# Decode on 16 bit words, value splits and finish moved, a later stack, six exponential places

## The reference

```
x = x + 0.5 * ffn(layernorm(x)); x = x + attention(layernorm(x)); x = x + 0.5 * ffn(layernorm(x))
ffn: w_gu, w_down = fp4 values (8 in an int32, table 0 .5 1 1.5 2 3 4 6 and signs) * fp16 scales per 128
     h = silu(x @ gate.T) * (x @ up.T)  (1408 wide);  y = h @ w_down.T;  y / sqrt(mean(y*y) + 1e-6)
attention: another layer norm with gain and bias; Q, K, V = Xn @ W + b; 16 heads of 32;
     causal softmax(Q K.T / sqrt(32)) @ V;  @ Wo + bo
```

## Time and profile before

| | us |
|---|---|
| median of 3 runs | 2748.12 (2747.58 to 2749.52) |
| profiled execution | 2745.77, its span 2744.0 |
| PE busy | 2589.1 (94%) |
| DVE busy | 1935.7 (71%) |
| POOL busy | 1510.9 (55%) |
| ACT busy | 1475.2 (54%) |

### The profile page before, as it was taken

One profiled execution on the slowest core, in us unless ns is written; L12 is line 12 of the kernel. 1 busy time (PEld: TensorE's weight loads), 2 busy tenths in 40 slices (PEclk: granted clock), 3 DMA queues, 4 the chain that ended last, 5 costly groups with the idle time before them and its releaser, 6 DMA issues.

```text
span 2744.0 us, 39443 instructions
## 1 busy us (share of the span) xinstructions
PE 2589.1 (94%) x14559; PEld 1361.4 (50%) x14559; DVE 1935.7 (71%) x3379; ACT 1475.2 (54%) x2834; POOL 1510.9 (55%) x1061
## 2 busy tenths in 40 slices
PE   5799999999898999999999989999999999999998
PEld 3455555555673333333278723333334555555554
DVE  7987777767647877777475577777764877777765
ACT  3366666665323566666622246656665466666664
POOL 4556666665322566666342236666662556666665
PEclk8999999999999999999999999999999999999999
DMA  2002311121023020200050210202002501111101
GB/s 63 1 31 93 127 47 47 47 93 47 31 57 70 6 50 4 65 5 3 3 199 31 71 42 6 48 6 64 6 3 102 196 16 47 47 47 47 47 31 47
DMA packets 78016, 136.34 MB, mean 50 GB/s; under 512 B 19551, under 2 KB 24698, under 8 KB 77694
## 3 DMA queue, kind: packets, MB, share of 16 engines
q1 hardware_dynamic: 77822, 133.81, 15.7%
HBM read 71.12 MB, written 34.34 MB: 38 GB/s over the span
## 4 chain that ended last, share of the span: by engine, by line
PE 70%; DVE 11%; POOL 5%; ACT 5%; issue 4%; SPq 2%; DMA 1%; POOLq 0%; DVEq 0%; ACTq 0%
PE pp L96 55%; PE ps L96 14%; DVE sb L117 5%; POOL sb L105 5%; ACT sb L102 5%; DVE sb L111 4%; SPq L138 2%; PE ps L99 1%; DVE sb L105 1%; DVE sb L108 0%; DMA sb<-sb 0%; DMA sb<-xc 0%; PE pp L99 0%; DVE sb L123 0%; DVE sb L114 0%
## 5 line engine op out<-in xcount | busy, mean ns | idle before, releaser
L96 PE MATMUL pp<-sb,sb 128*128 128x512 f32 (+10 forms) x11128 | 2199.9, 439 | 64.3 <-DVE sb L105 15.1
L105 POOL TENSOR_TENSOR sb<-sb,sb 128x512 f32<-128x512 f32 (+6 forms) x1042 | 1503.2, 1464 | 1220.4 <-ACT sb L102 422.2
L96 PEld LDWEIGHTS pp<-sb,sb 128*32 128x32 f32 (+4 forms) x11128 | 1076.0, 131 | 930.5 <-issue 369.6
L102 ACT ACTIVATE sb<-pp 128x512 f32<-128x512 f32 (+5 forms) x1394 | 667.1, 550 | 457.9 <-PE pp L96 427.7
L96 PE MATMUL ps<-sb,sb 128*128 128x512 f16 (+7 forms) x2888 | 758.8, 350 | 59.0 <-DVE sb L111 22.3
L117 DVE TENSOR_REDUCE sb<-ps 128x1 f32<-128x512 f32 (+3 forms) x772 | 492.5, 668 | 151.2 <-PE ps L96 148.6
L102 ACT ACTIVATE sb<-sb 128x512 fp32r<-128x512 f32 (+4 forms) x515 | 308.5, 605 | 516.5 <-DVE sb L111 368.0
L96 PEld LDWEIGHTS ps<-sb,sb 128*128 128x128 f16 (+4 forms) x2888 | 241.0, 101 | 397.7 <-DVE sb L117 104.8
L111 DVE SCALAR_TENSOR_TENSOR sb<-ps,sb,sb 128x512 f32<-128x512 f32 x437 | 320.5, 748 | 132.1 <-PE ps L96 100.9
L111 DVE SCALAR_TENSOR_TENSOR sb<-pp,sb,sb 128x512 f32<-128x512 f32 x447 | 324.3, 746 | 109.2 <-PE pp L96 106.5
L117 DVE TENSOR_REDUCE sb<-pp 128x1 f32<-128x512 f32 (+3 forms) x348 | 232.6, 668 | 88.4 <-PE pp L96 87.9
(11 more groups left out here) (26 smaller groups left out, 398.0 us busy)
## 6 DMA issues: line engine op xcount, KB each, us to landing
sb<-sb SPq DMA_DIRECT2D x144, 128.0 KB, 2.4
sb<-L_attn_X SPq DMA_DIRECT2D x64, 256.0 KB, 3.4
sb<-xa SPq DMA_DIRECT2D x64, 256.0 KB, 4.6
sb<-xc SPq DMA_DIRECT2D x64, 256.0 KB, 3.5
xa<-sb SPq DMA_DIRECT2D x32, 256.0 KB, 2.0
xc<-sb SPq DMA_DIRECT2D x32, 256.0 KB, 5.1
out<-sb SPq DMA_DIRECT2D x32, 256.0 KB, 2.0
dd<-sb SPq DMA_DIRECT2D x11, 512.0 KB, 5.7
```

The source lines that it names most:

```text
L96: return self.e.matmul(*a, **k) if self.e else self
L102: return self.e.activation(*a, **k) if self.e else self
L105: return self.e.tensor_tensor(*a, **k) if self.e else self
```

## The change

Six edits. (1) `decode_dve` works on 16 bit words with immediates, and the mask constants and their wait go. (2) In batch 0 the four splits of Wv stand ahead of the tail's squares. (3) The finish of the last tile of the first feed-forward part is one fused VectorE instruction for each block of 128 tokens, as it already was in the second part; `features_dve` waits for it. (4) The second stack comes behind the rows of query tile 1 on SP's list, not of query tile 0. (5) ScalarE's keep waits for the stacks of its own head group alone. (6) From step 120 on, exponentials have six places, two of them in memory that the stack of head group 2 used; the first use of these waits for the last exponential of head group 2.

```diff
-    u = p.pk[:, :, :].rearrange("p a b -> p (a b)").bitcast(U32)[:, 192 * i:192 * i + 192]
+    u = p.pk[:, :, :].rearrange("p a b -> p (a b)").bitcast(U16)[:, 384 * i:384 * i + 384]
-            e.scalar_tensor_tensor(p.t1[m % 2][:, :].bitcast(U32), u, 12 - 4 * m, sign, ALU.logical_shift_left,
-                                   ALU.bitwise_and).then_inc(*p.V.up())
+            e.tensor_scalar(p.t1[m % 2][:, :], u, 12 - 4 * m, 0x8000, ALU.logical_shift_left,
+                            ALU.bitwise_and).then_inc(*p.V.up())
...
-            e.scalar_tensor_tensor(p.vv[:, m, half].bitcast(U32), u, abs(sh), size,
+            e.tensor_scalar(p.vv[:, m, half], u, abs(sh), 0x0E00,
...
-            e.scalar_tensor_tensor(v, v, 0, p.t1[(m - 1) % 2][:, :].bitcast(U32), ALU.logical_shift_left,
-                                   ALU.bitwise_or).then_inc(*p.V.up())
+            e.tensor_tensor(v, v, p.t1[(m - 1) % 2][:, :], ALU.bitwise_or).then_inc(*p.V.up())
...
-        elif what == "last" and not f.final(at[0]):
+        elif what == "last" and at[0] < NT - 1:
...
-        elif what == "last" and f.final(at[0]):
+        elif what == "last" and at[0] == NT - 1:
...
-            e.scalar_tensor_tensor(x, f.Y[tb], p.r4[:, tb:tb + 1], x, ALU.mult, ALU.add).then_inc(
+            e.scalar_tensor_tensor(x, f.Y[tb] if f.ph else p.ysb[tb][:, :], p.r4[:, tb:tb + 1], x, ALU.mult, ALU.add).then_inc(
...
+        if b == 0:
+            yield from (("split", 2, c) for c in range(KC))
         yield from (("tail", x) for x in tail[0])
-        beside = {1: [("tail", x) for x in tail[1] + tail[2]] + [("norm", 1)] * 8,
-                  4: [("split", 2, 0), ("split", 2, 1)], 5: [("split", 2, 2)], 6: [("split", 2, 3)]}
+        beside = {1: [("tail", x) for x in tail[1] + tail[2]] + [("norm", 1)] * 8}
+        if b:
+            beside.update({4: [("split", 2, 0), ("split", 2, 1)], 5: [("split", 2, 2)], 6: [("split", 2, 3)]})
...
+    def place(self, n):
+        g = 3 * len(self.steps) // 4
+        if n < g:
+            return n % NE, n - NE
+        i = (n - g) % (NE + 2)
+        return i, n - NE - 2 if n >= g + NE + 2 else g - NE + i if i < NE else None
...
-                if ev == ("rows", 0, 0):
+                if ev == ("rows", 0, 1):
                     out.append(("stack", 1))
...
-                for i in range(2):
-                    for j in range(4):
-                        e.wait_ge(*t.stacked[i][j].at((b, hg if hg % 2 == i else max(hg - 1, i))))
+                for j in range(4):
+                    e.wait_ge(*t.stacked[hg % 2][j].at((b, hg)))
```

More of the change, by code:

```diff
@@ L9 @@
 U16 = mybir.dt.uint16
-U32 = mybir.dt.uint32
 ALU = mybir.AluOpType
@@ L187, in constants @@
         self.two14 = take([128, 4], F32, 16)
-        self.masks = take([128, 4], U16, 16)
         self.st = take([128, 4, 6], F32, 96)
@@ L301, in __init__ @@
         self.isd_made, self.rms_made, self.y_scaled = (p.sign(n + x) for x in ("isd_made", "rms_made", "y_scaled"))
-        self.final_out = p.sign(n + "final_out") if ph else None
+        self.final_out = p.sign(n + "final_out")
         self.ring, self.Y = Ring(p.b[0:4]), p.b[4:8]
@@ L627, in decode_dve @@
     half = slice(384 * (i % 2), 384 * (i % 2) + 384)
-    u = p.pk[:, :, :].rearrange("p a b -> p (a b)").bitcast(U32)[:, 192 * i:192 * i + 192]
-    sign, size = (p.masks[:, 2 * j:2 * j + 2].bitcast(U32).broadcast_to([128, 192]) for j in range(2))
-    if i == 0:
-        e.wait_ge(*p.set_signals.at("masks"))
+    u = p.pk[:, :, :].rearrange("p a b -> p (a b)").bitcast(U16)[:, 384 * i:384 * i + 384]
     e.wait_ge(*f.pk_in.at("all"))
@@ L637, in decode_dve @@
             e.wait_ge(*p.V.now())
-            e.scalar_tensor_tensor(p.t1[m % 2][:, :].bitcast(U32), u, 12 - 4 * m, sign, ALU.logical_shift_left,
-                                   ALU.bitwise_and).then_inc(*p.V.up())
+            e.tensor_scalar(p.t1[m % 2][:, :], u, 12 - 4 * m, 0x8000, ALU.logical_shift_left,
+                            ALU.bitwise_and).then_inc(*p.V.up())
             yield
             sh = 9 - 4 * m
-            e.scalar_tensor_tensor(p.vv[:, m, half].bitcast(U32), u, abs(sh), size,
-                                   ALU.logical_shift_left if sh >= 0 else ALU.logical_shift_right,
-                                   ALU.bitwise_and).then_inc(*p.V.up(("bits", i, m)))
+            e.tensor_scalar(p.vv[:, m, half], u, abs(sh), 0x0E00,
+                            ALU.logical_shift_left if sh >= 0 else ALU.logical_shift_right,
+                            ALU.bitwise_and).then_inc(*p.V.up(("bits", i, m)))
             yield
         if m >= 1:
-            v = p.vv[:, m - 1, half].bitcast(U32)
+            v = p.vv[:, m - 1, half]
             e.wait_ge(*p.V.at(("bits", i, m - 1)))
-            e.scalar_tensor_tensor(v, v, 0, p.t1[(m - 1) % 2][:, :].bitcast(U32), ALU.logical_shift_left,
-                                   ALU.bitwise_or).then_inc(*p.V.up())
+            e.tensor_tensor(v, v, p.t1[(m - 1) % 2][:, :], ALU.bitwise_or).then_inc(*p.V.up())
             if m == 4:
@@ L886, in ffn_sp @@
             tt, tb = at
-            e.wait_ge(*(f.final_out if f.final(tt) else f.x_out).at((tt, tb)))
+            e.wait_ge(*(f.final_out if tt == NT - 1 else f.x_out).at((tt, tb)))
             e.dma_start(f.dst[tt, tb], p.xr[tb][:, :]).then_inc(*f.stored.up(tt))
@@ L1131, in features_dve @@
     if b == 0 and f == 2:
-        e.wait_ge(*p.f[0].x_out.at((NT - 1, 0)))
+        e.wait_ge(*p.f[0].final_out.at((NT - 1, 0)))
     e.tensor_copy((p.qs, p.ks)[n][:, f, 0, 512 * tt:512 * tt + 512], q.q32[s][:, :]).then_inc(
@@ L1176, in __init__ @@
         o = QS0 + 65536
-        self.E = [p.at([128, 4, 512], F32, o + 8192 * i) for i in range(NE)]
+        self.E = [p.at([128, 4, 512], F32, x) for x in [o + 8192 * i for i in range(NE)] + [QS0 + 98304, QS0 + 106496]]
         o = KP0 + 16384
@@ L1460, in att_pe @@
                 k = e.matmul(AV[32 * j:32 * j + 32, off:512], p.v[:, kt, 32 * h:32 * h + 32],
-                             t.E[n % NE][:, j, off:512], start=kt == 0, stop=kt == 4 * qt + 3)
+                             t.E[t.place(n)[0]][:, j, off:512], start=kt == 0, stop=kt == 4 * qt + 3)
             k.then_inc(*t.av_done.up((b, n)))
@@ L1470, in att_pe @@
             for j in range(4):
-                k = e.matmul(RS[32 * j:32 * j + 32, off:512], p.ones[:, :], t.E[(n - 1) % NE][:, j, off:512],
+                k = e.matmul(RS[32 * j:32 * j + 32, off:512], p.ones[:, :], t.E[t.place(n - 1)[0]][:, j, off:512],
                              start=kt == 1, stop=last)
@@ L1511, in att_act @@
             e.wait_ge(*t.sc_done.at((b, n, j)))
-            if n >= NE:
-                m = n - NE + 1 if n % 2 == 0 else n - NE
-                e.wait_ge(*t.sum_done.at((b, m)))
+            place, m = t.place(n)
+            if m is None:
+                e.wait_ge(*t.exp_done.at((b, t.last_step(2), 3)))
+            elif m >= 0:
+                e.wait_ge(*t.sum_done.at((b, m + 1 - m % 2)))
             else:
                 e.wait_ge(*p.qkv.proj_done.at((b, "values", 3, 3)))
-            e.activation(t.E[n % NE][:, j, off:512], p.b[r][:, off:512], ACT.Exp).then_inc(
+            e.activation(t.E[place][:, j, off:512], p.b[r][:, off:512], ACT.Exp).then_inc(
                 *t.exp_done.up((b, n, j)))
@@ L1601, in add_steps @@
         e.wait_ge(*t.exp_done.at((b, n, 2 * h + 1)))
-        x = t.E[(n - 1) % NE][:, c, off:512]
-        e.tensor_tensor(x, x, t.E[n % NE][:, c, off:512], ALU.add).then_inc(*made.up((b, n, h)))
+        x = t.E[t.place(n - 1)[0]][:, c, off:512]
+        e.tensor_tensor(x, x, t.E[t.place(n)[0]][:, c, off:512], ALU.add).then_inc(*made.up((b, n, h)))
 def att_pool(e, p, b):
```

2 lines of the change are left out of this document (removed).

## The result

| us | before | after | after, timed again |
|---|---|---|---|
| median | 2748.82 | 2715.74 | 2704.45 |
| single runs | 2747.58 to 2750.58 | 2697.42, 2711.28, 2720.2, 2720.43 | 2697.17, 2699.36, 2709.54, 2710.95 |
| ratio to before, interval | | 0.9867 [0.9818, 0.9915] | 0.9845 [0.9825, 0.9865] |

The change makes the kernel 1.3 to 1.6% faster. The forecast was 2716 with 2699 to 2738. Ratios and intervals are taken over the runs at the usual granted clock (0.985 and more); one run of an experiment, 2819.2 us at a clock of 0.894, stands outside them. The runs of the kernel after now differ by 23 us; those of before differ by 3 in this comparison, by 9 in the longest one (17 runs, 2742.19 to 2751.5) and by 11 in another (9 runs, 2745.15 to 2755.96). The profiled execution of after took 2711.28, its span is 2709.5 against 2744.0.

A forecast was written before the change was run, and what follows sets the result against it. TensorE, 70% of the chain, was taken to bound the kernel, so edits pay only where it idles or runs at its lower clock. Decode 2, value splits 8, stack 10 and places 12 sum to 32: 2748.1 to 2716 us, range 2699 to 2738.

The forecast's parts named there:

- Decode (2 us): Decoding: 16 bit words shorten VectorE's twelve instructions a chunk from 3.7 to 3.2 us alone; together 2 us gained.
- They end about one to each GpSimd instruction: Decode chunks 2 to 10: VectorE's first five finish at GpSimd's pace, so only their own length shrinks, some 1.3 us.
- rival (c): Decoding: one-source instructions pass GpSimd by, 20 us gained in place of 2, 2698 us; chance 0.08.
- decode chunks keep 13.5 us: Sign of being right, in decoding; chunks at 15 us or more, or at 11, would show it wrong.
- rival (d): Decoding: one-source and GpSimd's instructions block each other in turn, 60 us lost, 2778 us; chance 0.06.
- Value splits and finish (8 us): Start of the first batch's projections: TensorE's 10.86 us of idling become about 4; 8 us gained.
- needs the four normalizations: Projections' start: TensorE's first transpose of tile 1 waits for all four normalizations, forecast at 707.3, range 706 to 709.
- Rival (e): Projections' start: the value gap isn't closed, another wait takes its place, 2724 us; chance 0.08.
- Stack and keep (5 a batch): Attention's start: row copies ahead of the second stack remove TensorE's wait; 5 us a batch, 10 in sum.
- would otherwise grow to some 20 us: Attention's start: ScalarE's first keep waited 3.5 us for the second stack; unchanged, the later stack would lengthen that.
- Six places (6 a batch): Last 16 attention steps: pairs of steps shrink from 5.47 to 4.5 us; 6 us a batch, 12 in sum.
- Rival (a): Last attention steps: TensorE is the bound and six places give nothing, 2728 us; chance 0.12.

The follow-up runs named there:

- add_waits: Kernel after with GpSimd's second instruction of a decode chunk waiting for VectorE's first five decode instructions, the other seven behind quarter 3: 2693.54 us, ratio 0.9801.

## Why the prediction was right

**The sum** was 32; the profiled executions differ by 34.5. The agreement of the median with 2716 is partly luck: the second comparison gives 2704.45, and all eight runs together 2710. Both lie in the range.

**Decode (2 us).** This term was mis-sized, and it was no single number. Alone, an instruction costs about what I took: 0.87 / 4 = 0.22 and 0.35 against 0.25 and 0.31, 3.1 a chunk against 3.2. "They end about one to each GpSimd instruction" holds in the long pattern. What I had as rival (c), that they no longer meet GpSimd, at 0.08, came true in part: in some executions, for four or five chunks, by a gap of GpSimd's of 0.6 us. Against the 32 bit decode in the same surroundings the term is 6.4 by trace in the long pattern and some 18 in the short one. The first profile shows 0.6 because the profiled execution of before had short chunks (11.2, 11.9 and 12.7) of its own. The step that failed is "they end about one to each GpSimd instruction, so only their own length shrinks", taken for every chunk alike. In the short pattern they do not meet the row; and I priced VectorE's instruction but not what TensorE does with its release, which is to start at one clock or the other. In the long pattern "decode chunks keep 13.5 us" nearly held (13.2), and of its 6.4 us 3.6 had come by the start of chunk 4's decoding. The short one, 10.5, is what I had named as a sign of being wrong.
The estimate of 2.3 us a chunk from the Trainium skill (VectorE: DVE Perf Modes, "The perf-mode tier table") was too low: 0.16 and 0.26 stood against 0.22 and 0.35. The rule of full blocking in the Trainium skill (SBUF — State Buffer, "Who interferes with whom") is met on VectorE's side: each of its four ends with one GpSimd instruction (1.26 and 1.28). GpSimd's five were not lengthened by them (6.40, 1.28 each, as in add_waits where it runs its four in 5.11), so rival (d) did not come.

**Value splits and finish (8 us).** 8.5 usually, 10.1 in the first profile. The first normalization starts at 703.75, where it started at 703.00. The projections themselves began 0.66 earlier in this execution, so that is 1.4 later against the forecast 1.6: VectorE's finish is through at 698.3, and three tiny instructions take 0.58 where they took 3.01. What I had wrong is that the first transpose "needs the four normalizations": it went behind the first, at 704.44, and not at 707.3. So the idle time was nearer 3 than 4, and "TensorE was at the lower clock for 3 us and lost 1.6" held in all executions but one. The splits bring 7.2 to 8.7, the finish 0.3. Rival (e) did not come.

**Stack and keep (5 a batch).** 6.8 and 5.5 in the first comparison, 6.4 and 5.8 undone. In batch 0 the idle time of 5.6 went whole, where I took 4.5 of it, and 1.2 more came in the slow stretch behind it, where I allowed 0.5. That the kept wait "would otherwise grow to some 20 us" was right in kind: 17.4 for ScalarE, 14 for the kernel.

**Six places (6 a batch).** 5.5 each in the first comparison; undone, 5.4 to 7.2. Pairs came out 4.60 apart (forecast 4.5) and the gap 0.57. Rival (a) was wrong: the 33 us that held 30.64 of TensorE's modelled busy time now take 27.6, so at least 3 of the 30.64 were not real.

## What to carry to other kernels

When an engine is "busy" for 5 us with four instructions that take 0.9 alone, look at what runs beside them: here it was GpSimd's row, and who queued behind them paid. Try holding back the other engine for the microsecond that the short ones need; here moving the short ones along the list brought less. When a kernel's runs fall on two levels, compare one trace of each, chunk by chunk: a pattern can repeat itself, and forcing the better one may be worth more than the change that uncovered it (2710 to 2694 us here). A wait that covers a neighbour's buffer too can cost little until something moves: before moving a transfer later, look for every wait that includes it.

## What the runs showed of the hardware

- The same idle time gives different clocks. In the two executions of after, TensorE stood 1.95 + 0.90 and 1.94 + 0.90 us; the 12 matmuls behind took 3.02 and 4.59. At step 144 it stood 1.24 in both, and 32 matmuls took 5.03 in the first and 3.33 in the second: 1.6 to 1.7 us each time, between two executions of one kernel. The granted clock is the last but two of a window's numbers (0.50 and 1.00).
```profile
1307.75 0.60 PE L95 MATMUL ps<-sb,sb 128*128 128x384 f16 x4 [1.24 <-ACT sb L101]
1308.28 5.03 PE L95 MATMUL pp<-sb,sb 128*32 128x512 f32 x32
...
1309.00:1311.00 2.00, 2.00 (x16) 0.64 (x12) 0.00 (x0) 0.04 (x1) 0.82 (x1) 0.50 0.09 21
```
```profile
1308.89 0.60 PE L95 MATMUL ps<-sb,sb 128*128 128x384 f16 x4 [1.24 <-ACT sb L101]
1309.42 3.33 PE L95 MATMUL pp<-sb,sb 128*32 128x512 f32 x32
...
1309.00:1311.00 2.00, 2.00 (x20) 0.70 (x22) 0.00 (x0) 0.87 (x2) 0.40 (x1) 1.00 0.16 39
```
- In add_waits VectorE's evictions from PSUM run beside GpSimd undisturbed (two in 1.51 us, 0.74 each with nothing beside them), while two one-source instructions on halfwords in SBUF take 1.15 to 1.45 there against 0.43 alone (after, at 14.88).
- What stays open: the two runs of after at 2720, ten above the profiled one, have no trace, and the decode patterns account only for 2697 and 2710.
